# Attention of a small transformer block, per batch on small float32 tiles

## What is computed

```python
x = x + attn(cond(x, lengths, ...), Wq, Wk, Wv, Wo)
x = x + ffn(mix_channels(x, weights[condition]), W_base, gate_W, A, B)

def attn(h, Wq, Wk, Wv, Wo):        # 32 query heads, 8 key heads, 32 features each
    q, k, v = heads(h @ Wq.T), heads(h @ Wk.T), heads(h @ Wv.T)
    k, v = repeat(k, 4), repeat(v, 4)
    q, k = rope(q), rope(k)
    scores = q @ k.T / sqrt(32) + causal_mask        # 64 x 64 for a batch and head
    return heads_joined(softmax(scores) @ v) @ Wo.T
```

## Time and profile before

| | us |
|---|---|
| median of 3 runs | 998.98 |
| lowest, highest | 998.18, 1000.43 |
| the profiled execution, its time | 999.68 |
| its span in the profile | 997.9 |

### The profile page before, as it was taken

How to read it: one execution, slowest core, us unless ns; L and a number is a source line. 1 busy time by engine, 2 the same in 40 slices (tenths; PEclk the granted TensorE clock), 3 DMA queues, 4 the chain that set the end, 5 groups by cost and what they waited for, 6 DMA issues and landing times.

```text
span 997.9 us, 19473 instructions
## 1 busy us (share of the span) xinstructions
PE 936.2 (94%) x7984; PEld 829.5 (83%) x7984; DVE 500.9 (50%) x967; ACT 287.2 (29%) x509; POOL 364.6 (37%) x264
## 2 busy tenths in 40 slices
PE   0999999899999999994899999999999999999997
PEld 0889899898888888883688888888878999999997
DVE  6555651002545454556676666666644343343344
ACT  4345542011111112135444445354341110110110
POOL 1244564104666666556455555554411000000000
PEclk9999999999999999997899999999999999999999
DMA  2687777012336454449754453635164212212111
GB/s 78 151 216 188 189 187 192 22 43 69 121 116 159 122 132 106 106 128 253 189 166 156 146 179 125 200 109 190 43 241 130 81 47 85 79 50 85 65 43 64
DMA packets 120949, 125.97 MB, mean 126 GB/s; under 512 B 75424, under 2 KB 90400, under 8 KB 120864
## 3 DMA queue, kind: packets, MB, share of 16 engines
q1 hardware_dynamic: 120352, 124.22, 43.3%
q0 software_dynamic: 512, 0.53, 0.2%
HBM read 84.57 MB, written 40.14 MB: 125 GB/s over the span
## 4 chain that ended last, share of the span: by engine, by line
PE 83%; DVE 5%; DMA 4%; POOL 3%; ACT 2%; SPq 2%; issue 1%; DVEq 0%; POOLq 0%
PE ps L744 19%; PE ps L1239 18%; PE ps L997 16%; PE ps L498 8%; PE ps L727 5%; PE ps L940 4%; PE ps L509 4%; PE ps L1207 3%; PE ps L954 3%; PE ps L974 2%; DMA wstage<-in_dram 2%; DMA kpad<-ksb 1%; POOL rf L827 1%; PE ps L1259 1%; PE ps L1260 1%
## 5 line engine op out<-in xcount | busy, mean ns | idle before, releaser
L1239 PE MATMUL ps<-wb,xf 128*128 128x420 f32 (+1 forms) x1152 | 195.7, 329 | 2.4 <-DVE wb L1292 1.6
L1239 PEld LDWEIGHTS ps<-wb,xf 128*128 128x128 f32 x1152 | 189.3, 188 | 6.0 <-issue 3.4
L744 PE MATMUL ps<-y_hi,w_hi 128*128 128x512 f32 x320 | 124.5, 389 | 0.0
L744 PE MATMUL ps<-y_lo,w_hi 128*128 128x512 f32 x320 | 124.5, 389 | 0.0
L744 PE MATMUL ps<-y_hi,w_lo 128*128 128x512 f32 x320 | 124.5, 389 | 0.0
L498 PE MATMUL ps<-xc,toep 64*128 64x192 f32 (+4 forms) x1088 | 100.3, 336 | 13.0 <-DMA toep<-kpad 8.3
L997 PE MATMUL ps<-wo_hi,ot_hi 128*128 128x512 f32 x256 | 107.4, 419 | 0.0
L498 PEld LDWEIGHTS ps<-xc,toep 64*128 64x128 f32 x1088 | 92.2, 191 | 17.4 <-issue 11.8
L997 PE MATMUL ps<-wo_hi,ot_lo 128*128 128x512 f32 x256 | 101.3, 396 | 0.0
L997 PE MATMUL ps<-wo_lo,ot_hi 128*128 128x512 f32 x256 | 100.9, 394 | 0.0
L1034 POOL TENSOR_TENSOR sc<-sc,stat 128x1024 f32<-128x1024 f32 x32 | 62.0, 1938 | 63.9 <-DVE stat L1030 63.9
(11 more groups left out here) (152 smaller groups left out, 1528.0 us busy)
## 6 DMA issues: line engine op xcount, KB each, us to landing
toep<-kpad SPq DMA_DIRECT2D x64, 272.0 KB, 5.0
xc<-in_dram SPq DMA_DIRECT2D x32, 256.0 KB, 5.3
q_hi<-stg_hi SPq DMA_DIRECT2D x32, 256.0 KB, 2.6
q_lo<-stg_lo SPq DMA_DIRECT2D x32, 256.0 KB, 3.4
q<-q_hi SPq DMA_DIRECT2D x16, 512.0 KB, 5.7
q<-q_lo SPq DMA_DIRECT2D x16, 512.0 KB, 6.4
xr<-in_dram SPq DMA_DIRECT2D x16, 512.0 KB, 4.6
x_scratch<-xr SPq DMA_DIRECT2D x16, 512.0 KB, 3.0
```

Source lines behind the costliest of these rows:

```text
L744: mm = pe.matmul(ps[:, 4 * (m % 2) + g, :], w[a][:, j, :], yt[b][:, j, g * 512:(g + 1) * 512], start=(j == 0 and a + b == 0), stop=(j == N ...
L1239: mm = pe.matmul(joint_bank(i, piece)[:, 0:hi - lo], xf[i % 2][:, a, t, :], wb[t][:, c, lo:hi], start=(t == 0 and a + c == 0), stop=(piece ...
```

## The change

The attention is laid out anew:

- q and k are not split. They are stored, loaded and used as float32. `k_bd`, `place_k` and the zeroing of it go; so do the splits in `qkv_hi` and `qkv_rope`.
- `scores` has 32 float32 matmuls of 64 columns on 32x64 tiles (a head's 32 features are the rows, 64 queries the columns of a tile) and writes the first 256 columns of PSUM banks 0 to 3.
- The probabilities are turned by VectorE, in blocks of 32x32, straight from `sc` to `pt`. The transposes on TensorE and the copies from PSUM go.
- `values` has 24 float32 matmuls on 32x32 tiles with 128 columns, and leaves out the blocks that the causal mask makes zero. Its moving operand is read with a step of 64 elements. `ot` is laid out by token and then by head of a group, so the stationary operand of `project` is read with a step of 4.
- `project` is cut in pieces of 8, 10 and 6 matmuls, with the values after the first and the scores of batch `w + 3` after the second. The waits for the output weights are there in the first half only.
- Scores run three batches ahead (`CR = 3` slots of `sc` instead of 2). Scores of batches 0 and 1 come before tiles `(Z, 2)` and `(Z, 3)` of the projections.
- ScalarE copies the projection from PSUM to `pr`, and GpSimd adds the residual (`take_projection`, `add_residual`).
- GpSimd's gather comes after the product of a batch and before the subtraction of the next.
- An output weight tile is loaded with one DMA. The feed-forward weight tiles 0 to 3 are loaded and split in steps 22 to 28, tiles 4 and 5 in steps 32 and 33.

The core of the diff:

```diff
-            for G in range(NG):
-                for rp in range(2):
-                    for a, c in PASSES:
-                        mm = pe.matmul(ps[:, G, rp * 256:(rp + 1) * 256],
-                                       q_sb[i % 2][:, a, b, G * REP + 2 * rp:G * REP + 2 * rp + 2, :],
-                                       k_bd[i % 2][:, c, b, G, :], start=(a + c == 0), stop=(a == 1))
+            for rep in range(REP):
+                for G in range(NG):
+                    for g in range(4):
+                        rows = slice(g * HD, (g + 1) * HD)
+                        mm = pe.matmul(ps[G * S:(G + 1) * S, g, rep * S:(rep + 1) * S], q_sb[i % 2][rows, b, G * REP + rep, :],
+                                       kc[rows, i % 2, G, b * S:(b + 1) * S], start=True, stop=True)
...
         def values(pe, u):
+            pe.wait_ge(v_pt, u + 1)
+            pe.wait_ge(v_sc, min(u + CR, NUNIT))
...
+            probs = pt[:].rearrange("p (g r j q) -> p g j q r", g=4, r=REP, j=2)
+            for j in range(2):
+                for quad in range(4):
+                    G, late = quad // 2, quad % 2
+                    if j > late:
+                        continue
+                    rows = slice(quad * HB, (quad + 1) * HB)
+                    for g in range(4):
+                        mm = pe.matmul(ps[g * HD:(g + 1) * HD, quad, 256:384], vc[rows, i % VR, b, j, g * HD:(g + 1) * HD],
+                                       probs[rows, g, j, :, :], start=(j == 0), stop=(j == late))
...
+        STOPS = (0, 8, 18, 24)
+
+        def project(pe, i, n, piece):
...
+            for at in range(STOPS[piece], STOPS[piece + 1]):
+                t, (a, c) = at // 3, PASSES[at % 3]
+                if i + n == 0 and at % 3 == 0:
+                    wo_split(pe, t)
+                heads = ot[a][:, i % 2, t // REP, :, :, t % REP].rearrange("p h q -> p (h q)")
...
         def attention_matmuls(pe):
-            scores(pe, 1)
+            scores(pe, 2)
             pe.wait_ge(v_rcos, 4 * NU)
+            for w in STEPS:
+                i, n = w // 2 - 1, w % 2
+                if i >= 0:
+                    project(pe, i, n, 0)
+                if w < NUNIT:
+                    values(pe, w)
...
+                if i >= 0:
+                    project(pe, i, n, 1)
+                if w + CR < NUNIT:
+                    scores(pe, w + CR)
                 if i >= 0:
+                    project(pe, i, n, 2)
...
+        def turn_probs(v, u):
+            v.wait_ge(g_prob, u + 1)
+            if u > 0:
+                v.wait_ge(pe_o, u)
+            v.transpose(pt[:], sc[:, u % CR, :]).then_inc(v_pt, 1)
...
         def attention_softmax(v):
+            for w in STEPS:
...
+                if w < NUNIT:
+                    v.wait_ge(a_othi, w + 1)
+                    v.tensor_tensor(o_heads(1, w), o_banks(), o_heads(0, w).bitcast(F32), ALU.subtract).then_inc(v_otlo, 1)
+                if w + 1 < NUNIT:
+                    turn_probs(v, w + 1)
+                if w + 2 < NUNIT:
+                    sums(v, w + 2)
+                if w + CR < NUNIT:
+                    scale_and_max(v, w + CR)
+                for t in WO_LO_V.get(w, ()):
+                    wo_lo(v, t)
...
         def attention_scale(gp):
+            for w in range(NUNIT + 3):
+                u = w + 2
+                if 3 <= u < NUNIT:
                     subtract_max(gp, u)
+                if w >= 3:
+                    add_residual(gp, (w - 1) // 2 - 1, (w - 1) % 2)
+                if u < NUNIT:
+                    normalise(gp, u)
```

More of the change, by code:

```diff
@@ L190, in build, with fill, take @@
[L190 to L194, removed]
+        def fill(stack, name, upto):
+            sb(name, [P, upto - sum(used[stack])], F32, stack)
+            used[stack].append(upto - sum(used[stack]))
+        used = {}
+        def take(stack, name, shape, dt=F32):
+            used.setdefault(stack, []).append(int(np.prod(shape[1:])))
+            return sb(name, shape, dt, stack)
@@ new lines, in build @@
+        cidx_i = take(s3, "cidx_i", [P, NB], I32)
+        cidx = take(s3, "cidx", [P, NPAIR], U32)
+        KEEP_TO = sum(used[s3])
+        fill(s3, "rest_of_y", Y_END)
+        pt = take(s3, "pt", [P, 1024])
+        q_1 = take(s3, "q_1", [P, 2, NQT, S])
+        take(s3, "last_raw_weights", [P, L])
+        WS3 = 4
+        wstage3 = [take(s3, f"wstage3_{n}", [P, L]) for n in (0, 1)]
+        take(s3, "last_hi_weights", [P, L])
+        wstage3 += [take(s3, f"wstage3_{n}", [P, L]) for n in (2, 3)]
@@ L214, in build @@
-        sb("rest_of_wo", [P, 2 * NQT * L - late], F32, s4)
-        WS4 = 3
[L217 to L224, removed]
+        bexp_hi = take(s4, "bexp_hi", [2 * NH, L], F32R)
@@ L225, in build @@
+        WB_FREE = 4
+        wb = [take(s4, f"wb_{t}", [P, 2, NBASE], F32R) for t in range(WB_FREE)]
+        x1 += [take(s4, "x1_1", [P, L])] + x1_late
+        fill(s4, "rest_of_rope", Q_AT)
+        wb += [take(s4, f"wb_{t}", [P, 2, NBASE], F32R) for t in range(WB_FREE, WB_EARLY)] + wb_late
+        xf = [take(s4, "xf_0", [P, 2, NJ, P], F32R), xf_late]
         s4.close()
@@ L663, in next_weights, with stores_up_to, stored @@
             return Z if n == 4 * A - 2 else n // 4 + 1 if n % 4 == 0 and n // 4 + 1 < Z else None
+        def stores_up_to(n):
+            return 16 * sum(2 if k < NVB else 1 for k in range(n % SR, n + 1, SR))
+        def stored(eng, n):
+            eng.wait_ge(st_stg[n % SR], stores_up_to(n))
         def qkv_transfers(sp):
@@ L925, in attention_transfers @@
                         load_residual(sp, i + 1)
-            for t in range(WS4, WB_EARLY):
+            for t in range(WS4 + 1, WB_EARLY):
                 load_w4(sp, t)
@@ L1010, in attention_matmuls @@
                 if i >= 0:
-                    project(pe, i, 2 * k)
-                for part in (values, scores) if w < 2 else (scores, values):
-                    u = w if part is values else w + 2
-                    if u < NUNIT:
-                        part(pe, u)
+                    project(pe, i, n, 1)
+                if w + CR < NUNIT:
+                    scores(pe, w + CR)
                 if i >= 0:
-                    project(pe, i, 2 * k + 1)
+                    project(pe, i, n, 2)
```

473 lines of the change are left out of this document (190 added, 283 removed).

## The result

The changed kernel takes 1006.23 us (median of 4 runs, 1005.95 to 1006.78), the kernel before 999.7 us beside it: 1.0068 times as long, 95% interval 1.005 to 1.0085. It is slower by 0.7%; the forecast was 963 us. The profiled execution took 1006.78 us. The kernel before ran beside each group of experiments too (medians 998.5 to 1000.7 us), so kernels of different groups are to be compared by their ratio to it; where no ratio is given, a kernel ran once and only its profile is read.

What follows compares the result with a forecast made beforehand. TensorE was taken to bound the kernel before, and a softmax ring after: 999.68 - 32.4 (29 steps) - 1.5 (last steps) - 2.4 (start-up) = 963.4, median 963 us; range 948 to 990.

Steps and rivals of the forecast that it cites:

- For the values I take none: Value matmuls: the strided read of the probabilities costs nothing; double, +0.5 us a step, kept for the range.
- Rival 2: Value matmuls: strided probabilities cost the absolute pace of ScalarE's row, TensorE's step 8.4 us, kernel 988; chance 0.11.
- The stationary operand: Output projection: its strided load, 0.23 us, can hide behind the matmul in front, so no cost.
- Rival 3: Output projection: strided stationary loads stop hiding, 0.21 us more per matmul, kernel 1104; chance 0.09 together with another rival.
- The burst of short instructions: Attention step on TensorE: 64 score instructions take 0.52 us, 48 value instructions 0.60 us.
- The upper end: Score matmuls: 1.04 us by columns, instead of 0.52 with eight tiles working instead of four.
- The passages: TensorE between tile shapes in a step: 0.11 us more at the values, 0.3 us in all at the scores.
- The ring: Softmax from one batch's maximum to the next's, binding next: 7.15 us a step, 7.75 with a gather.
- The start-up: Start of attention, from the last projection tile to step 3: 38.3 us, 2.4 us saved.
- The low clock: Start of attention: another 1.5 us for TensorE's low clock after waits.
- Rival 5: Attention steps: GpSimd and VectorE block each other, the block transpose waits, sums come 0.1 us later: +3 us.
- The block transpose: VectorE in each step, 1024 elements: 1.2 us, at most 2.4 at half rate.

Runs made afterwards that it cites:

- by_rep: Changed kernel with both TensorE reads contiguous and tokens in right order, batch outputs written strided in two instructions instead of one: 973.57 us, ratio 0.9759.
- gather_late: rep_vector_lows with GpSimd's gather behind the subtraction of the maximum, not ahead of it: 965.68 us, ratio 0.9677.
- rep_vector_lows: by_rep with batch 1's outputs ahead of the high parts of tiles 4 to 7 on ScalarE, all low parts on VectorE: 972.99 us, ratio 0.9724.
- scores_wide: by_rep with the same 64 score instructions, but 48 of them with 128 columns instead of 64: 978.02 us.
- moving_step_2: by_rep with the value matmuls reading 128 probabilities at a step of 2 elements, 8 bytes: 976.81 us.
- moving_contiguous: Changed kernel with probabilities read 32 adjacent elements at a time, the projection's stationary operand keeping its step of 4: 983.67 us, ratio 0.9858.

## Why the prediction was wrong

Its sum for one step of TensorE, against the traces (the projection pieces include the passages from shape to shape):

| us per step | forecast | after | both reads contiguous |
|---|---|---|---|
| values, start to next | 0.60 | 1.59 | 0.86 |
| scores, start to next | 0.52 | 0.84 | 0.84 |
| 24 projection matmuls, passages | 5.86 | 6.28 | 5.89 |
| sum | 6.98 | 8.71 | 7.59 |

- **The step that failed** is "For the values I take none", and the same for the stationary operand: two strided reads that were put at no cost. Of the 1.73 us missing, 1.12 are these two strides: 0.73 and 0.39. The prediction held both as rivals. Rival 2 priced the moving operand at +1.4 us, 988 us for the kernel, and had a chance of 0.11; measured is +0.73. (By its own terms, 243.6 against 217.0, it is 990.) Its argument against itself, that TensorE only reads, is refuted: reads pay too. Of the signs that the prediction names for being wrong, the value burst over 0.7 us came; the spacing of the projection matmuls stayed at 0.235 us and the block transpose at 1.23.
- **The stationary operand** was argued to hide behind the matmul in front. Between like matmuls it does (0.006 us left); behind a burst, where nothing long is in front, its 313 ns stand open. Rival 3 had the right place with the wrong size: it forecast 24 x 0.21 us, measured are two exposed loads of 0.127 us and 20 times 0.006. It put the point where the gain is gone at 0.295 us per matmul; it was gone at 0.235, since the other terms had used up the margin.
- **The burst of short instructions** is the second mis-sized term. Scaling by columns and tiles gave 0.52 and 0.60 us; without any stride it is 0.84 and 0.86, +0.58 us a step. The convolution row, on which this was built, has 20 ns per instruction on four tiles; halving it for eight tiles was a choice. The upper end named in the text, 1.04 (64 x 20 x 0.8 is 1.02), bounds the 0.84 measured. The passages were right within 0.03 us.
- **The ring** was right, and not where the time went. Measured 7.68 with a gather, forecast 7.75; without one 6.94, forecast 7.15. In after it stays hidden behind TensorE's 8.72, and its signs (VectorE waiting for the exponential, steps in two groups) appear only where TensorE is made faster. The forecast let the ring bind because it held TensorE's own step to be 6.98; even with both reads contiguous that is 7.59, above the 7.48 that it took for the ring in the mean.
- **The steps in all**: 29 x (8.72 - 7.48) = 36 us over the forecast (217.0 / 29 = 7.48).
- **The start-up** was forecast at 38.3 us, as 2.4 us saved; it is 47.4. (Both end where step 3 begins, which after is matmul 25; before, step 3 begins with its transposes, at 40.7, and matmul 25 comes at 41.8.) The mis-sized term is the low part on VectorE: 1.25 us taken, 3.3 in the mean measured, 1.21 alone but 7.33 and 5.52 beside GpSimd. Tile 4 is thus issued 22.9 us after the last q projection matmul, not 16, and the outputs of batch 1 come at 28.8, not 24. The low clock was sized about right: some ten of the first 24 projection matmuls start 0.43 instead of 0.235 us apart, about 1.9 us against the 1.5 allowed. Rival 5 named the mechanism and placed it in the steady steps, between subtraction and block transpose, at +3 us. There all transposes take 1.23 or 1.24 us; of the steady steps only the four with a weight split on VectorE show it (in by_rep the subtraction takes 2.89 instead of 1.92 us). The start-up shows it in full. With low parts on VectorE alone, ScalarE's order turned and the gather moved, the start-up takes 37.7 us, close to the 38.3.
- **The block transpose** was 1.2 us, measured 1.23. GpSimd's residual add, at most 1.5, is 1.3. The q, k, v projections are unchanged (218.6 against 219.2), and the end of attention to the end of the kernel takes 247.2 us against 247.7.

36 + 9 us (47.4 against 38.3) is 45, less some 1.6 in the last steps and the stages around; the kernel missed the forecast by 43. With the causes undone, the version gather_late takes 965.7 us, 3 us from the number forecast. That is no confirmation of the sum: TensorE's 7.60 takes the place of the ring's 7.48, and the start-up was reached by other means than the change has. And that number was given for the kernel with the strides; for it the range, 948 to 990, didn't hold: its upper end carried rival 2 alone, although stride and low parts have independent causes and can come together. With the forecast's own prices that sum is 990 + 6, near 996, and with scores at 1.04 us 1011.

## What to carry over

A read of TensorE that stepped by 16 bytes or more cost time in both operands here, so it is to be written into the sum; choose the layout so that TensorE reads adjacent elements and an engine off the path does the reordering, which here took two writes instead of one (2 x 0.38 us on ScalarE instead of 0.58) and nothing of the kernel's time. Count short matmuls as well as their columns, and expect each burst to expose the first weight load behind it. Where two tensor operations on VectorE and GpSimd split one job, check that they are faster together than one alone.

## What was not expected of the hardware

- 48 value instructions of 128 float32 columns: 0.86 us contiguous, 0.88 at a step of 8 bytes, 1.30 at 16, 1.59 in after's read of 4 elements at 256. The Trainium skill (SBUF — State Buffer, "Door 1: The DMA port swizzle") wants two hits on a 16-byte line for full bandwidth, and the free step of 8 bytes agrees; that 4 float32 can be stridden for free doesn't: 16 bytes cost half as much again.
- A 128x128 float32 weight load: 188 ns contiguous, 313 ns at a step of 16 bytes.
- On bursts of 32x64 and 32x32 tiles, 9.2 ns per instruction and 0.062 ns per column, taken from two score bursts, give a third (0.42 us) and nearly the values (0.82, measured 0.86), but not before's 16 longer instructions (0.40, measured 0.59).
- VectorE's subtraction of 1024 elements from two operands in SBUF: 1.21 us alone, 7.33 beside three operations in a row on GpSimd (after), ending 1.1 us behind the last of them.
- In rep_vector_lows and moving_step_2 value bursts that begin some 0.5 us into a gather of GpSimd take 1.0 to 1.2 us instead of 0.86; in by_rep and scores_wide bursts at a like distance don't. GpSimd's subtraction beside a burst leaves it at 0.86. With strided values that subtraction is itself slowed: 1.98 to 2.45 us beside such a burst in after (2.15 at 601.87), 1.90 to 1.92 beside a contiguous one in moving_contiguous, the steps with a weight split left out.
